# Down projections of the feed-forward blocks turned round: whole-number weights stationary, gated units in two halves moving, transposed back; bank table and written-out order lists

## The chip, the core and the metric

The kernel runs on one core of one Trainium2 chip. The metric is the device time of one execution in microseconds (us), the median of several. The engines are TensorE (PE, with its weight loads as PEld), VectorE (DVE), ScalarE (ACT), GpSimd (POOL) and SyncE (SP), which issues most DMAs. Each engine runs its own instructions in the order in which they are written, and waits at semaphores for the others.

## What is computed

The input x holds 8 sequences ("batches" below) of 256 rows with 128 features. Four residual blocks follow one another, each on a layernorm of x: a first attention without softmax (A), a feed-forward block (F), a causal softmax attention with 16 heads of 64 (B), and the same feed-forward block again (P, with the same weights). Cut down:

```python
x = x + attn_a(layernorm(x))     # sigmoid projections, signed exp(-|dt|) weights, @ V @ Wo
x = x + ffn(layernorm(x))        # "F"
x = x + attn_b(layernorm(x))     # 16 heads, causal softmax, "B"
x = x + ffn(layernorm(x))        # "P"

def ffn(x):                      # w_*: whole numbers from -127 to 127, scaled by 1/127
    gate, up = x @ wg.T, x @ wu.T            # 128 -> 384 each
    return (silu(gate) * up) @ wd.T          # 384 -> 128
```

All is in float32. The down projection, the product with `wd`, is what the change is about.

## The kernel before

**Tiles.** A batch is 256 rows, two tiles of 128 (`T = 2`). After each layernorm the normalised rows are transposed on PE (job `lntA`, `lntF`, `lntB`, `lntP`, line 300) and kept with features on partitions, as a high half in the fp32r format (ACT, line 489) and the rest, the low half (DVE, line 671). fp32r products need one pass of PE over the moving columns for each instruction, so most projections are sums of products of halves: `qkv` (block A) and `qk`, `v` (block B) of three (`split3`, lines 280 to 282), the gate and up products `gF0..2`, `gP0..2` of two, since the whole-number weights are exact in one half (lines 342 and 343). The rest is plain float32, which the trace shows as two PE records for each product: `mean` (313, 315), `vwo` (323), `aout` (331), scores (418, 420), the sums of values (454), `out0/out1` (384), and the down projections `dnF`, `dnP` (line 352). Heads are taken in pairs, `m` from 0 to 63, eight pairs for a batch.

**Down projection.** `gF0..2` give, for a third of the 384 units each, gate and up in one PSUM bank. ACT takes tanh of the gate (512), DVE makes `gated` (676) and `hid` (679). For each of the two row tiles `dnF` then takes the columns of `hid` as the stationary operand, three of 128x128, and streams `wd` (128 columns, float32): six products, twelve records. The result has rows on partitions, and DVE adds it to x straight from PSUM (650).

**Attention B, one pair of heads.** `qk` on PE, DVE adds the bias (722), `scores` on PE, DVE masks and takes the maximum (696, 698), ACT takes exp (543, 545), DVE the inverse of the sums (712), POOL normalises (`norm`, 798), PE transposes the probabilities (432), ACT and DVE copy them out (552, 705), and PE forms the weighted sums (454), two pairs at a time.

**Order.** `order(engine)` gives each engine its list of jobs. It is a table of numbers: steady places per pair of heads (`HEADS`) and per batch (`JOBS`), with places of their own for the first batches (`FIRST`), the last ones (`FINAL`) and single jobs (`ONCE`); the list is sorted by them. Batches overlap: while B of batch b runs, A and F of the next batches and P of the last one are put between its pairs of heads. `hot` and `end` jobs are four products of the identity with itself, that nobody reads.

**Banks.** PSUM has eight banks. Four are fixed for the attention, two for scores and two for transposed probabilities, and the other jobs share four by the table `BANK`: all `qk` use one bank and all `sum` the same one. `take` makes PE wait until the last user of the bank is done (`g_free`); `full` and `freed` are waits for a bank written or emptied.

Of the kernel before, what the change touches and what calls it, by code (L numbers as in the profile page):

```python
# [21 lines left out]
P = 128  # L22
ALU = mybir.AluOpType
# [6 lines left out]
H, A = 16, 64  # L30
# [17 lines left out]
HEADS = {  # L48
    "PE": {"qk": (-1.47, -1.62856), "scores": (0.0, -0.833), "transposes": (1.99091, 1.19991), "sum": (3.2, 3.14491)},
    "ACT": {"exp0": (0.23441, -0.21159), "exp1": (0.28441, -0.20059), "pt0": (2.07727, 1.29991), "sum": (3.3, 3.24991)},  # L50
    "DVE": {"qk": (-0.5119, -0.63388), "mask": (0.708, 0.228), "inverse": (1.29732, 1.34732), "pt1": (2.71379, 2.82508)},
    "POOL": {"norm": (5.06245, 4.32791)},
}
JOBS = {
    "PE": {"lntA": -13.6156, "qkv0": -12.26453, "qkv1": -10.64958, "qkv2": -10.30138, "mean": -10.13088, "vwo": -9.72583,
           "aout": -9.10583, "lntF": -7.70714, "gF0": -6.78825, "gF1": -5.78525, "gF2": -5.72825, "dnF": -4.7632, "lntB": -2.16884,
           "v0": -1.55034, "v2": 1.06591, "v1": 1.20257, "v3": 4.88788, "out0": 10.5084, "out1": 13.1196, "lntP": 14.58389,
           "gP0": 15.43388, "gP2": 15.922, "gP1": 19.74527, "dnP": 23.94389},
    "ACT": {"lntA": -13.17167, "qkv0": -13.0559, "qkv1": -10.76319, "qkv2": -10.2456, "dist": -9.90133, "vwo": -9.70983,
            "lntF": -7.53195, "gF0": -5.89131, "gF1": -5.34525, "gF2": -5.30283, "lntB": -2.36166, "v0": -1.25162, "v2": 1.67502,  # L60
            "v1": 2.21014, "v3": 5.60312, "lntP": 14.41869, "gP0": 15.53771, "gP2": 16.02125, "gP1": 19.2699},
    "DVE": {"lnsA": -21.82637, "lntA": -11.8, "mean": -9.39079, "sign": -9.09363, "aout": -8.43983, "lnsF": -7.98053, "lntF": -6.51241,
            "gF0": -5.20042, "gF2": -4.66206, "gF1": -4.63025, "dnF": -3.78101, "lnsB": -3.68499, "lntB": -1.24016, "out0": 12.0634,
            "out1": 13.89046, "lnsP": 13.97249, "lntP": 15.50477, "gP2": 16.5658, "gP0": 16.76417, "gP1": 20.95233, "dnP": 24.54168},
    "POOL": {"lnsA": -17.39504, "sv": -5.80262, "stdp": -4.98145, "lnsF": -4.33472, "lnsB": 0.17439, "bo": 6.18821, "lnsP": 18.15549},
}
ONCE = {
# [773 lines left out]
```

## Time and profile before

| | us |
|---|---|
| median of 3 runs | 344.57 (344.52 to 344.84) |
| span of the profiled execution | 342.4 |
| what lies around the span (median less span) | 2.2 |
| PE busy | 329.4 |
| DVE busy | 264.8 |
| ACT busy | 231.6 |
| POOL busy | 200.0 |

The profiled execution has no time of its own beside its span; the median is set against that. Matmuls are pipelined, so the busy time of PE counts overlapping ends; how fast it goes is read from the distance between the starts of its instructions in the timeline.

### The profile page before, as it was taken

The numbers are of one execution on the slowest core, as the hardware profiler recorded it, in microseconds if no ns is written. First come the engines' busy times: TensorE is split into PE (matmuls) and PEld (weight loads), VectorE is DVE, ScalarE is ACT, GpSimd is POOL, SyncE is SP. The second block draws the span as 40 slices with busy tenths as digits, with TensorE's granted clock in tenths as the row PEclk, the third lists the DMA queues.
The fourth block names the chain that finished last, engine by engine and source line by source line (L and its number), as shares of the span: only waits on it lengthen the run. The fifth ranks groups of instructions, "written<-read, shape, count | busy, mean of one in ns | idle before, by whom it ended". The sixth has DMA issues, their size and how long they took to land.

```text
span 342.4 us, 10121 instructions
## 1 busy us (share of the span) xinstructions
PE 329.4 (96%) x3344; PEld 284.3 (83%) x3344; DVE 264.8 (77%) x1092; ACT 231.6 (68%) x784; POOL 200.0 (58%) x265
## 2 busy tenths in 40 slices
PE   6899899999999999999999999999999999999985
PEld 5788697779888888889988888888898888888875
DVE  4566799779889798898788788887787886877553
ACT  2544676986788767685786767685787757866711
POOL 4566587477676677557657667634658265444600
PEclk9999999999999999999999999999999999999999
DMA  7800000000000000000000000000000000000001
GB/s 207 278 3 0 3 0 4 2 2 4 0 2 4 2 0 3 17 3 1 2 3 19 0 2 4 15 2 3 3 0 18 2 3 15 3 2 3 16 2 31
DMA packets 6418, 5.83 MB, mean 17 GB/s; under 512 B 864, under 2 KB 5856, under 8 KB 6368
## 3 DMA queue, kind: packets, MB, share of 16 engines
q1 hardware_dynamic: 6080, 4.99, 4.9%
q8 instruction: 27, 0.44, 0.5%
q10 hardware_dynamic: 288, 0.20, 0.2%
q14 instruction: 23, 0.19, 0.2%
HBM read 4.15 MB, written 1.05 MB: 15 GB/s over the span
## 4 chain that ended last, share of the span: by engine, by line
PE 76%; POOL 8%; issue 7%; DVE 5%; ACT 2%; DMA 1%; DVEq 0%; POOLq 0%
PE bank L454 11%; PE bank L280 7%; PE bank L432 7%; PE bank L420 7%; PE bank L384 7%; PE bank L282 6%; PE bank L281 6%; PE bank L418 6%; PE bank L352 5%; PE bank L342 4%; PE bank L343 3%; PE bank L300 2%; POOL prob L798 2%; PE bank L331 2%; POOL wqkv_lo L785 1%
## 5 line engine op out<-in xcount | busy, mean ns | idle before, releaser
L798 POOL TENSOR_TENSOR prob<-prob,row_inv 128x256 f32<-128x256 f32 (+1 forms) x128 | 103.1, 826 | 90.1 <-DVE row_inv L712 90.1
L545 ACT ACTIVATE prob<-neg_s,neg_max 128x256 f32<-128x256 f32 x128 | 63.7, 498 | 0.0
L543 ACT ACTIVATE prob<-neg_s,neg_max 128x128 f32<-128x128 f32 x128 | 50.5, 394 | 17.8 <-DVE neg_max L698 17.2
L698 DVE CUSTOM_DVE_ANT_0 neg_s<-bank,mask 128x256 f32<-128x256 f32 x128 | 53.6, 419 | 0.0
L722 DVE TENSOR_TENSOR qk<-bank,bqk 128x512 f32<-128x512 f32 x64 | 44.0, 688 | 11.9 <-PE bank L282 10.9
L454 PE MATMUL bank<-prob_t,v 128*64 128x256 f32 (+1 forms) x512 | 48.7, 332 | 0.2
L454 PEld LDWEIGHTS bank<-prob_t,v 128*64 128x64 f32 x512 | 32.0, 136 | 19.5 <-ACT prob_t L552 9.7
L696 DVE CUSTOM_DVE_ANT_0 neg_s<-bank,mask 128x128 f32<-128x128 f32 x128 | 36.6, 286 | 13.6 <-PE bank L420 13.1
L552 ACT ACTIVATE prob_t<-bank 128x384 f32<-128x384 f32 x64 | 30.9, 482 | 19.7 <-PE bank L432 18.9
L280 PE MATMUL bank<-rt_hi,wqkv_hi 128*128 128x256 f32 x128 | 39.9, 312 | 0.3
L420 PE MATMUL bank<-qk 64*128 64x256 f32 x256 | 38.5, 377 | 0.0
L432 PEld LDWEIGHTS bank<-ident,prob 64*128 64x128 f32 x768 | 31.8, 139 | 7.4 <-POOL prob L798 0.9
L432 PE MATMUL bank<-ident,prob 64*128 64x64 f32 x768 | 36.0, 226 | 0.4 <-DVE prob_t L705 0.4
L705 DVE COPY prob_t<-bank 128x384 f32<-128x384 f32 x64 | 35.2, 549 | 1.6 <-PE bank L432 1.6
L282 PE MATMUL bank<-rt_lo,wqkv_hi 128*128 128x256 f32 x128 | 35.8, 280 | 0.0
L281 PE MATMUL bank<-rt_hi,wqkv_lo 128*128 128x256 f32 x128 | 35.8, 280 | 0.0
L418 PE MATMUL bank<-qk 64*128 64x128 f32 x256 | 29.9, 310 | 1.1 <-DVE neg_max L698 0.9
L500 ACT ACTIVATE t_qkv<-bank,ga_bias,ga_scale 128x256 f32<-128x256 f32 x24 | 13.4, 562 | 24.4 <-PE bank L282 24.4
L384 PE MATMUL bank<-wo,zt 128*128 128x128 f32 x232 | 28.3, 275 | 0.0
L384 PEld LDWEIGHTS bank<-wo,zt 128*128 128x128 f32 x232 | 27.3, 192 | 0.2
L280 PEld LDWEIGHTS bank<-rt_hi,wqkv_hi 128*128 128x128 f32 x128 | 24.1, 189 | 2.6 <-DVE qk L722 1.2
L418 PEld LDWEIGHTS bank<-qk 64*128 64x128 f32 x256 | 19.6, 187 | 6.7 <-issue 6.5
(145 smaller groups left out, 795.0 us busy)
## 6 DMA issues: line engine op xcount, KB each, us to landing
wqkv<-wqkv_in SPq DMA_DIRECT2D x3, 512.0 KB, 7.1
x<-x_in SPq DMA_DIRECT2D x8, 128.0 KB, 5.7
out<-x SPq DMA_DIRECT2D x8, 128.0 KB, 1.8
wo<-wo_in SPq DMA_DIRECT2D x1, 512.0 KB, 6.8
wa<-wa_in ACTq DMA_DIRECT2D x1, 192.0 KB, 3.0
wg_i<-wg_in SPq DMA_DIRECT2D x1, 192.0 KB, 3.4
wu_i<-wu_in SPq DMA_DIRECT2D x1, 192.0 KB, 3.5
wd_i<-wd_in SPq DMA_DIRECT2D x1, 192.0 KB, 5.0
```

What stands on the lines that cost most here:

```text
L280: nc.tensor.matmul(out, w_hi_ap, r_hi_ap, start=True, stop=False)
L281: nc.tensor.matmul(out, w_lo_ap, r_hi_ap, start=False, stop=False)
L282: return nc.tensor.matmul(out, w_hi_ap, r_lo_ap, start=False, stop=True)
L384: last = nc.tensor.matmul(out[:, 0:D], zt[:, b % 2, u, j * P:(j + 1) * P], wo[:, u, :], start=(u == 0), stop=(u == U - 1))
L418: nc.tensor.matmul(s_banks[e][:, 0:P], qk[half, r, 0, 0:P], qk[half, r, 1, 0:P], start=True, stop=True)
L420: nc.tensor.matmul(s_banks[e][:, P:SC], qk[half, r, 0, P:N], qk[half, r, 1, :], start=True, stop=True).then_inc(s_full, 1)
L432: last = nc.tensor.transpose(t_banks[h][:, at:at + A], prob[half, m % 4, e, j * P:(j + 1) * P], ident[half, half])
L454: last = nc.tensor.matmul(out[half, t + k * P:t + N], v[:, b % 2, k, h * A:(h + 1) * A], prob_t[:, i % 4, e, cols], start=(k == 0), stop=( ...
L543: nc.scalar.activation(prob[:, r, e, 0:P], neg_s[:, m % 2, e, 0:P], ACT.Exp, bias=neg_max[:, q, 2 * e:2 * e + 1], scale=-1.0, accum_out=ro ...
L545: nc.scalar.activation(prob[:, r, e, P:SC], neg_s[:, m % 2, e, P:SC], ACT.Exp, bias=neg_max[:, q, 2 * e + 1:2 * e + 2], scale=-1.0, accum_ ...
L698: nc.vector.tensor_tensor_reduce(out=neg_s[:, m % 2, e, P:SC], in0=S[:, P:SC], in1=mask[:], scale=-SCORE_SCALE, scalar=3e38, op0=ALU.add, ...
L798: nc.gpsimd.tensor_tensor(pr, pr, inv, ALU.mult).then_inc(p_norm, 1)
```

## The change

The down projections of batches 1 to 7 in F and of 0 to 6 in P (14 of 16) are turned round. `wd`, now held in fp32r, is the stationary operand, and `hid`, split in two fp32r halves, moves: three products of 128x256 for the high half and three for the low half. The split is new work: ACT writes `hid_hi` (job `hh`, 768 columns), POOL subtracts and writes `hid_lo` (job `hl`, 768 columns). The result now has features on partitions; ACT copies it out of PSUM (`dnt`, 256 columns), and a new PE job `dbF`/`dbP` transposes it back, two of 128x128. DVE's addition to x is as before, from the bank of `db`. The first of F and the last of P keep the old form, under the name `db` (`DIRECT`). `hid` is made in place, without `gated`.

Every bank of every job now stands in a table (`BANKS`, one digit for each use), the scores, transposes and `hot` jobs too, and `take` holds for all of them. The orders are written out as lists for each engine (`ORDER`), different all over. The last P uses the buffers of F. There are 18 `hot` jobs in place of 28 `hot` and 6 `end`.

```diff
-JOBS = {
-    "PE": {"lntA": -13.6156, "qkv0": -12.26453, "qkv1": -10.64958, "qkv2": -10.30138, "mean": -10.13088, "vwo": -9.72583,
...
+ORDER = {
+    "PE": """
+        lntA.0 hot.0 hot.1 qkv0.0 qkv1.0 qkv2.0 mean.0 hot.2 lntA.1 hot.3 vwo.0 hot.4 qkv1.1 aout.0 qkv0.1 hot.5 hot.6 mean.1
+        lntF.0 hot.7 hot.8 gF2.0 gF1.0 gF0.0 qkv2.1 bo.0 lntA.2 dbF.0 hot.9 qkv2.2 vwo.1 qkv1.2 qkv0.2 aout.1 lntB.0 hot.10
+        hot.11 qk.0 v0.0 qk.1 scores.0 scores.1 lntF.1 qk.2 qk.3 gF1.1 gF0.1 v3.0 gF2.1 v1.0 qk.4 scores.2 scores.3 scores.4
...
+BANKS = {
...
+    "s0": "3116444442011212746107166024553565711005607344543114072352206173",
+    "s1": "0472076114725337263476243276330606300221422060617720267037635360",
...
+DIRECT = {("F", 0), ("P", B - 1)}
...
+        def turn_of(k, b):
+
+            return b + 1 - (k == "F")
+
+        def buffers(k, b):
+
+            return "F" if (k, b) == ("P", B - 1) else k
...
                 elif job in ("dnF", "dnP"):
                     k = job[2]
-                    for c in range(FC):
-                        freed(pe, f"g{k}{c}", b)
+                    pe.wait_ge(hl_s[k], turn_of(k, b))
                     take(job, b)
-                    for j in range(T):
+                    for half in (hid_hi, hid_lo):
                         for c in range(FC):
-                            last = nc.tensor.matmul(out[:, j * D:(j + 1) * D], hid[k][:, c, j * P:(j + 1) * P], wd[:, c, :],
-                                                    start=(c == 0), stop=(c == FC - 1))
+                            last = nc.tensor.matmul(out[:, 0:N], wd[:, c, :], half[k][:, c, :], start=(half is hid_hi and c == 0),
+                                                    stop=(half is hid_lo and c == FC - 1))
+                    last.then_inc(done, 1)
+                elif job in ("dbF", "dbP"):
+                    k = job[2]
+                    if (k, b) in DIRECT:
...
+                    else:
+                        freed(pe, f"dn{k}", b)
+                        take(job, b)
+                        for j in range(T):
+                            last = nc.tensor.transpose(out[:, j * D:(j + 1) * D], dnt[k][:, 0, j * P:(j + 1) * P], ident[:])
                     last.then_inc(done, 1)
...
             def scores(m):
 
                 freed(pe, "qk", m)
-                if m:
-                    pe.wait_ge(s_masked, 2 * m)
+                take("s0", m)
+                take("s1", m)
...
+                elif job in ("hhF", "hhP"):
+                    k = job[2]
+                    for c in range(FC):
+                        freed(act, f"g{k}{c}", b)
+                    if turn_of(k, b) > 1:
+                        full(act, f"dn{k}", b - 1)
+                    nc.scalar.activation(hid_hi[k][:], hid[k][:], ACT.Copy).then_inc(hh_s[k], 1)
+                elif job in ("dnF", "dnP"):
...
+                    nc.scalar.activation(dnt[k][:, 0, :], src[:, 0:N], ACT.Copy).then_inc(free, 1)
...
+                elif job in ("hlF", "hlP"):
+                    k = job[2]
+                    pool.wait_ge(hh_s[k], turn_of(k, b))
+                    if turn_of(k, b) > 1:
+                        full(pool, f"dn{k}", b - 1)
+                    nc.gpsimd.tensor_tensor(hid_lo[k][:], hid[k][:], hid_hi[k][:].bitcast(F32), ALU.subtract).then_inc(hl_s[k], 1)
```

Three places of the order. PE at the start of the program, before (L300 is `lntA.0`, L365 the `hot` jobs, the others are `qkv0`):

```order
L365 MATMUL bank<-ident 128x128 x24
L300 MATMUL bank<-ident,xn_A 128x128 x2
L365 MATMUL bank<-ident 128x128 x4
L280 MATMUL bank<-xt_hi_A,wa_hi 128x256
L281 MATMUL bank<-xt_hi_A,wa_lo 128x256
```

and after (L373 is `lntA.0`, L454 to L456 `hot`):

```order
L373 MATMUL bank<-ident,xn_A 128x128 x2
L454 MATMUL bank<-ident 128x128 x2
L455 MATMUL bank<-ident 128x128
L456 MATMUL bank<-ident 128x128
L454 MATMUL bank<-ident 128x128 x2
L455 MATMUL bank<-ident 128x128
L456 MATMUL bank<-ident 128x128
L355 MATMUL bank<-xt_hi_A,wa_hi 128x256
```

The 24 products ahead of the first transposes are gone; eight stand behind them.

PE about the down projection of F in batch 4 before (L352 is `dnF`, between two `qk`):

```order
L384 MATMUL bank<-wo,zt 128x128 x8
L280 MATMUL bank<-rt_hi,wqkv_hi 128x256
L281 MATMUL bank<-rt_hi,wqkv_lo 128x256
L282 MATMUL bank<-rt_lo,wqkv_hi 128x256
L280 MATMUL bank<-rt_hi,wqkv_hi 128x256
L281 MATMUL bank<-rt_hi,wqkv_lo 128x256
L282 MATMUL bank<-rt_lo,wqkv_hi 128x256
L352 MATMUL bank<-wd,hid_F 128x128 x6
L280 MATMUL bank<-rt_hi,wqkv_hi 128x256
```

and after (L424 is `dnF`, L441 `dbF`; between them a `qk`, behind them the probabilities' transposes L518):

```order
L541 MATMUL bank<-prob_t,v 64x128 x2
L424 MATMUL bank<-hid_hi_F,wd 128x256 x3
L424 MATMUL bank<-hid_lo_F,wd 128x256 x3
L355 MATMUL bank<-rt_hi,wqkv_hi 128x256
L356 MATMUL bank<-rt_hi,wqkv_lo 128x256
L357 MATMUL bank<-rt_lo,wqkv_hi 128x256
L355 MATMUL bank<-rt_hi,wqkv_hi 128x256
L356 MATMUL bank<-rt_hi,wqkv_lo 128x256
L357 MATMUL bank<-rt_lo,wqkv_hi 128x256
L441 MATMUL bank<-ident,dnt_F 128x128 x2
L518 MATMUL bank<-ident,prob 128x64 x12
```

Six products of another shape stand for the six, and the two back transposes follow one `qk` later.

POOL at the split of `hid` in F, batch 4, after (L913 is `norm`, L860 to L878 `lnsA`, L888 `sv`, L900 `hlF`); before, there is no such row:

```order
L913 TENSOR_TENSOR prob<-prob,row_inv 128x2x128
L913 TENSOR_TENSOR prob<-prob,row_inv 128x2x256
L900 TENSOR_TENSOR hid_lo_F<-hid_F,hid_hi_F 128x768
L913 TENSOR_TENSOR prob<-prob,row_inv 128x2x128
L913 TENSOR_TENSOR prob<-prob,row_inv 128x2x256
L860 TENSOR_TENSOR rstd_A<-var_A,minus_half 128x2
```

`hlF` stands between the `norm` of two pairs of heads, and the second of them waits for it.

## Rows read from the trace of the kernel before

**Rows 1.** The page: busy time of each engine, then 40 equal slices of the span.
```profile
PE 329.4 (96%) x3344; PEld 284.3 (83%) x3344; DVE 264.8 (77%) x1092; ACT 231.6 (68%) x784; POOL 200.0 (58%) x265
...
PE   6899899999999999999999999999999999999985
...
PEclk9999999999999999999999999999999999999999
```

**Rows 2.** Windows, PE alone: stretch, length, busy (instructions), granted clock, DMA share, GB/s.
```profile
60.00:308.00 248.00, 247.48 (x2613) 1.00 0.02 5
```

**Rows 3.** Windows, all engines: PE, PEld, DVE, ACT, POOL busy, then as above.
```profile
193.30:231.60 38.30, 38.30 (x402) 33.25 (x401) 31.20 (x129) 28.07 (x98) 24.32 (x32) 1.00 0.02 5
326.00:342.40 16.40, 11.57 (x96) 10.60 (x94) 7.93 (x24) 2.68 (x7) 0.72 (x1) 1.00 0.06 17
```

**Rows 4.** Timeline of PE about dnF.4: start, length, instruction, count.
```profile
195.57 1.50 PE L352 MATMUL bank<-wd,hid_F 128*128 128x128 f32 x12
196.82 0.36 PE L280 MATMUL bank<-rt_hi,wqkv_hi 128*128 128x256 f32 x1
197.03 0.28 PE L281 MATMUL bank<-rt_hi,wqkv_lo 128*128 128x256 f32 x1
197.15 0.28 PE L282 MATMUL bank<-rt_lo,wqkv_hi 128*128 128x256 f32 x1
```

**Rows 5.** Timeline of PE: two transposes of 128x128, aout, the next qk.
```profile
214.35 0.39 PE L300 MATMUL bank<-ident,xn_P 128*128 128x128 f32 x2
214.57 1.06 PE L331 MATMUL bank<-vwo,stdp 128*128 128x128 f32 x8
215.38 0.37 PE L280 MATMUL bank<-rt_hi,wqkv_hi 128*128 128x256 f32 x1
```

**Rows 6.** Groups by line and shape: count, busy, mean ns, idle time before.
```profile
L785 POOL TENSOR_TENSOR wqkv_lo<-wqkv,wqkv_hi 128x512 fp32r<-128x512 f32 x6 | 7.6, 1287 | 0.7 <-DVE xn_B L615 0.7
L524 ACT ACTIVATE wqkv_hi<-wqkv 128x512 fp32r<-128x512 f32 x6 | 3.6, 623 | 0.0
L489 ACT ACTIVATE xt_hi_P<-bank 128x256 fp32r<-128x256 f32 x8 | 3.1, 382 | 9.6 <-PE bank L300 9.4
```

**Rows 7.** Waits: who waited for whom, us in total, times, longest.
```profile
POOL prob L798 <- DVE row_inv L712: 90.1, 57, 4.4
```

**Rows 8.** Timeline: the last pair's scores on PE, and its normalisation on POOL.
```profile
317.02 0.49 PE L418 MATMUL bank<-qk 64*128 64x128 f32 x4
...
321.50 1.61 POOL L798 TENSOR_TENSOR prob<-prob,row_inv 128x256 f32<-128x256 f32 x2 [0.54 <-DVE row_inv L712]
```

**Rows 9.** Windows, PE alone, inside the first 24 hot products; columns as in rows 2.
```profile
2.90:3.90 1.00, 1.00 (x6) 1.00 0.93 264
...
4.90:5.90 1.00, 1.00 (x11) 1.00 0.84 252
```

**Rows 10.** Timeline, batch 0's chain and batch 1's mean: DVE and POOL.
```profile
12.18 0.75 DVE L635 TENSOR_SCALAR less<-tq,ntk 128x256 f32<-128x256 f32 x2
30.79 1.56 DVE L635 TENSOR_SCALAR less<-tq,ntk 128x256 f32<-128x256 f32 x2
...
14.37 0.81 POOL L770 TENSOR_TENSOR xb<-x,boa 128x256 f32<-128x256 f32 x1
15.27 0.94 POOL L791 TENSOR_SCALAR stdp<-signed 128x512 f32<-128x512 f32 x1
30.43 1.28 POOL L785 TENSOR_TENSOR wqkv_lo<-wqkv,wqkv_hi 128x512 fp32r<-128x512 f32 x1 [0.72 <-DVE xn_B L615]
```

**Rows 11.** Timeline of PE: lntA.0, lntB.0, the second pair's scores, lntP.7.
```profile
6.63 0.41 PE L300 MATMUL bank<-ident,xn_A 128*128 128x128 f32 x2 [0.44 <-DVE xn_A L615]
...
30.41 0.44 PE L300 MATMUL bank<-ident,xn_B 128*128 128x128 f32 x2
...
39.79 0.49 PE L418 MATMUL bank<-qk 64*128 64x128 f32 x4 [0.94 <-DVE neg_max L698]
...
332.82 0.44 PE L300 MATMUL bank<-ident,xn_P 128*128 128x128 f32 x2 [1.08 <-DVE xn_P L615]
```

More of the change, by code:

```diff
@@ L43 @@
 BIG = 1e30
[L48 to L52, printed above, removed]
-}
-JOBS = {
-    "PE": {"lntA": -13.6156, "qkv0": -12.26453, "qkv1": -10.64958, "qkv2": -10.30138, "mean": -10.13088, "vwo": -9.72583,
[L56 to L66, printed above, removed]
@@ new lines @@
+BANKS = {
+    "lntA": "51315605",
+    "qkv0": "15612257",
+    "qkv1": "77315641",
+    "qkv2": "26704630",
+    "mean": "12536726",
+    "vwo": "64761224",
+    "aout": "11142604",
+    "bo": "5",
+    "lntF": "06653573",
+    "gF0": "37203426",
+    "gF2": "45422673",
+    "gF1": "02644713",
+    "dbF": "71536147",
+    "lntB": "05174423",
+    "v1": "06565532",
+    "qk": "6103475323055467264574754747130452375345651647573151564250546145",
+    "v0": "35167174",
+    "s0": "3116444442011212746107166024553565711005607344543114072352206173",
+    "s1": "0472076114725337263476243276330606300221422060617720267037635360",
+    "v3": "13653451",
+    "t0": "6230235630412053022137541514237167663776751350420561121215173427",
+    "t1": "1351570727664502133450160647073242474040062761657643764147031565",
+    "dnF": "04524055",
+    "sum": "0000050000030706060501020001040202010304000700010001050102060706",
+    "v2": "64302267",
+    "out0": "63731140",
+    "out1": "35571723",
+    "lntP": "45452633",
+    "gP0": "00132611",
+    "gP2": "12345734",
+    "gP1": "12524047",
+    "dnP": "0627340",
+    "dbP": "71344730",
+    "hot": "020000012024000001",
@@ L120 @@
 }
 def order(engine):
-    steps = []
-    for name, at in HEADS[engine].items():
-        steps += [(m + at[m % 2], name, m) for m in range(LAST) if name != "sum" or m % 2]
-    for name, at in JOBS[engine].items():
-        first = FIRST[engine].get(name, ())
-        final = FINAL[engine].get(name, ())
-        places = list(first) + [U * b + at for b in range(len(first), B - len(final))] + list(final)
-        steps += [(place, name, b) for b, place in enumerate(places)]
-    for name, at in ONCE[engine].items():
-        steps.append((at, name, 0))
@@ L135, in order, with bank_of, users @@
-    return [(name, n) for _, name, n in sorted(steps)]
-LAST_BANK = {"out0": 4, "out1": 5, "lntP": 6, "gP0": 4, "gP1": 5, "gP2": 6}
-def bank_of(job, n):
-    return LAST_BANK[job] if n == B - 1 and job in LAST_BANK else BANK[job]
+    jobs = []
+    for place in ORDER[engine].split():
+        name, n = place.split(".")
+        jobs.append((name, int(n)))
+    return jobs
+def bank_of(user, n):
+    return int(BANKS[user][n])
+DIRECT = {("F", 0), ("P", B - 1)}
+def users(job, n):
+    if job == "scores":
+        return [("s0", n), ("s1", n)]
+    if job == "transposes":
+        return [("t0", n), ("t1", n)]
+    if job in ("pre0", "pre1"):
+        return [(job.replace("pre", "out"), B - 1)]
+    return [(job, n)]
@@ L147, in bank_turns @@
 def bank_turns():
     turns, count = {}, [0] * 8
-    for name, n in order("PE"):
-        if name in ("pre0", "pre1"):
-            name, n = name.replace("pre", "out"), B - 1
-        if name in BANK and (name, n) not in turns:
-            count[bank_of(name, n)] += 1
-            turns[name, n] = count[bank_of(name, n)]
+    for job, n in order("PE"):
+        for user in users(job, n):
+            if user not in turns:
+                count[bank_of(*user)] += 1
+                turns[user] = count[bank_of(*user)]
@@ L271, in _ @@
             for b in range(B):
-                freed(sp, "dnP", b)
+                freed(sp, "dbP", b)
                 sp.dma_start(out_view[:, b * T:(b + 1) * T, :], x[:, b * T:(b + 1) * T, :]).then_inc(stored, 16)
@@ L289, in side @@
             def side(job, b):
-                out, done, _ = home(job, b) if job in BANK else (None, None, None)
+                out, done, _ = home(job, b) if job in BANKS else (None, None, None)
                 if job.startswith("lnt"):
@@ L646, in side @@
                     nc.vector.tensor_tensor(x[:, ts, :], src[:, 0:N].rearrange("p (j d) -> p j d", d=D), xb[:, b % 2, :, :], ALU.add).then_inc(free, 1)
-                elif job in ("dnF", "dnP"):
+                elif job in ("dbF", "dbP"):
                     src, _, free = home(job, b)
@@ L690, in mask_max @@
                 for e in range(2):
-                    S = s_banks[e]
-                    dve.wait_ge(s_full, 2 * m + e + 1)
+                    S, _, free = home(f"s{e}", m)
+                    full(dve, f"s{e}", m)
                     if m >= 2:
```

260 lines of the change are left out of this document (168 added, 92 removed), and 13 rows, old and new, of tables (FINAL, ONCE).

## The prediction

> **What bounds the kernel now.** I read the page first. PE is busy for 96% of the span, in nearly every slice, at the full granted clock, and no other engine passes 77% [rows 1]. The windows by stretch say the same of the long middle: between 60 and 308 us PE lacks 0.5 us of 248 [rows 2], while in one batch's stretch of 38.3 us DVE works 31.2, ACT 28.1 and POOL 24.3 [rows 3]. So in the middle each us of PE work taken away is a us of time, as long as the others keep pace. Only the two ends have another limit. In the head, batch 0 has to go through blocks A and F before any heads can start (its `lntB.0` stands at 30.41 [rows 11]), and PE is filled with `hot` products. In the tail, from 326 us, PE is busy 11.6 of 16.4 us [rows 3]: the last P is a chain through all engines.
>
> **PE's prices** are distances between starts. A float32 down projection takes 1.25 us to the next start, and the first fp32r product behind it 0.09 more than its like (0.21 against 0.12) [rows 4], so 1.34 in all. An fp32r product of 256 columns takes 0.12 [rows 4]. Two transposes of 128x128 take 0.22 [rows 5]. `aout`, eight float32 records, takes 0.81, with the switch behind it 0.9 [rows 5].
>
> **Part 1, the turned down projections.** New cost of one: 6 x 0.12 = 0.72, and 0.22 for the transposes back. Of the 14 turned, 13 lie ahead of the tail (F 1 to 7, P 0 to 5), and 12 of their `db`; the others (`dnP.6`, `dbP.5`, `dbP.6`) lie in the tail in time in which PE waits for the last P. The sum: 13 x (0.72 - 1.34) = -8.1, and 12 x 0.22 = +2.6: **-5.5 us**. Bounds: if each `db` also brings a switch of 0.09, or one each way, it is -4.4 or -3.3; a gain beyond -5.5 needs a cheaper product than the like ones of `qk`, and no row has that. I take -5.5 since the float32 job that went had its switch too.
>
> **Part 2, what is moved ahead.** In the new order `lntA.2`, `vwo.1`, `aout.1` and `qkv0..2.2` stand ahead of `lntB.0`, where before they stood behind it (where PE is the limit) and `hot` products stood ahead. By the same prices: 0.22, four records of the down projection's kind 0.45 (4/12 of 1.34), 0.9, and 9 x 0.12 = 1.08. **-2.7 us**, hidden by the chain of batch 0. If that cover is too short, up to all of it comes back.
>
> **Part 3, banks.** Before, the second pair's scores waited 0.94 us until the first pair's bank was masked [rows 11]. The table now gives them banks of their own, and the two stand side by side: **-0.9 us**. In the middle PE had no waits worth counting [rows 2], so free banks bring nothing more there by themselves. `take` is one semaphore wait as before. Side by side, scores with scores and transposes with transposes, may save switches: adding up all prices of both lists from `lntB.0` to the last `out1` gives up to 1.0 us more for the new order than parts 1 and 2. No row shows two scores in a row; I leave it out of the sum and keep it for the range (0 to -1.0).
>
> **Part 4, the head.** Is `lntB.0` still at 30.4? For it: POOL now does batch 1's layernorm ahead of `sv.0`, so `stdp.0` is not held back by it. It began at 15.27, right behind batch 1's `xb` of 0.81 that ended at 15.18 [rows 10]: an estimated 0.6 earlier. Against it: DVE now does `mean.1`, whose `less` alone takes 0.75 to 1.56 [rows 10], between the norm and the low half of `lntF.0`, in part in time in which it waited before: an estimated +0.3 to +1.1. It also does `lnsA.2` and `bv` while the gates' tanh runs: about +0.5, half of which the three gates, now side by side, give back. And PE starts cold, next. Sum between -0.5 and +2; I take **+0.9 us**, the middle.
>
> The clock in the head: PE's first 24 `hot` products took some 0.17 us each before 3.9 us (6 in 1 us) and half of that at 4.9 (11 in 1 us), although the granted clock is given as 1.00 over both [rows 9]. So the array began at its lower level, 1.2 GHz, and rose while these ran. Without them it rises only behind `lntA.0`, at 6.63 or later [rows 11]: the transposes, eight `hot` and the first `qkv` at double price. The `hot` that stood between `qkv0` and `qkv1` is gone, which pays for most of it: 0.3 to 0.5, in the +0.9.
>
> **Part 5, work for the others.** ACT: `hh` has 768 columns; 512 took 0.62 and 256 0.38 [rows 6], so 0.86; `dnt` 0.38. 14 x 1.24 = 17 us over the run, 2.2 a batch: 28.1 to 30.3 of 37.3 us. POOL: `hl` by the like subtraction of 512 columns at 1.29 [rows 6] is 1.9 us; 14 of them 27 us, 3.5 a batch: 24.3 to 27.8. DVE is as before, 31.2 of 37.3. None reaches PE. What counts is what is queued behind. On POOL it is the next pair's `norm`, for which transposes on PE wait. POOL had waited 90.1 us in 57 places for the inverse [rows 7], 1.6 each: one `hl` eats that. The whole way from scores to the end of the normalisation was 317.02 to 323.11 = 6.1 us [rows 8]; with a full `hl` in front, 8.0. By the prices above, summed along the new list, PE has 7.2 to 16 us of other work between scores and transposes at the 13 pairs whose `norm` follows an `hl`, eleven of them over 8.3. From the last gate to `dn` PE has 5.4 us or more, against 0.8 on DVE (two steps of 256 columns, as the two `less` [rows 10]) + 0.9 + 1.9 = 3.6 and the semaphores. `dn` to `db` has 0.7 at its shortest, against 0.38 for the copy and two semaphores: just enough. I cost part 5 at **0**, at 0 to +5 for the range.
>
> **The shared port.** When POOL split a weight, `less` on DVE took 1.56 in place of 0.75 [rows 10]. The Trainium skill ("SBUF — State Buffer", section "Who interferes with whom") says that DVE in certain modes, or with two SBUF inputs, and POOL share one port pair as an exclusive lock, the loser waiting for the whole instruction; the trace agrees by these two rows. By that rule `hl` can hold DVE for up to 1.9 us with `qk` and `mask` behind. DVE has three such instructions a batch (two `less`, `signed`), and `hl` runs 3.5 of 37 us, so about 0.3 meet in a batch, some 0.3 us on an engine with 6 us to spare. It changes the bounds of part 5, not the sum.
>
> **Tail.** The last P keeps its form. `pre0` now stands ahead of the last `sum`, a mere exchange on PE. `dnP.6` (0.7) replaces an `end` in the wait between `lntP.7` (332.82 [rows 11]) and its gates. 0.
>
> **Sum.** -5.5 - 2.7 - 0.9 + 0.9 = -8.2 us: span 342.4 to 334.2, with the 2.2 around it **336.4 us**.
>
> **Rivals.** (a) The clock stays low through the head: with fewer `hot` the array is at work perhaps two thirds of the time there, and batch 0's own PE jobs (some 4.5 us at full clock from `mean.0` to `lntB.0`) take double: +4.5, of which 0.4 is counted and some falls into waits: +3.5, 339.9. For it: rows 9. Against it: in the tail PE was busy 70% of the time [rows 3] and the clock held. The Trainium skill ("TensorE: Matmul & The Clock Gate", section "What's actually happening") says that throttled is the default and activity releases it; by that the start is cold, as rows 9 show. (b) The in-order engines give part of it back: 14 splits with 0.3 us of PE wait each, +4.2: 340.6. For it: DVE at 84% and ACT at 81% of the time are no longer slack for every job. Against it: the distances above. (c) The same orders save the 1.0 us of switches, and the head comes out at -0.5 or better: -1.0 - 1.4 or a bit more, some 333.7. (d) The turned product doesn't do what it says: six products with their switches and the copy cost 1.3 after all. Then part 1 is 0 and it is 341.9. Nothing speaks for it, since the `qk` products of rows 4 have the same types. (e) **Slower than before:** POOL becomes the chain. Each `hl` is late by the wait for `hh` behind exps on ACT, and PE stands for all of the 1.9 us at each of 14 places and 0.3 after `dn`: +30 at most; it turns slower from 0.6 us at each (8.2 / 14). At 0.8 each and nothing else it is +3 over before: 347.6. Against it is the room of 7 to 16 us.
>
> **How the numbers follow.** The forecast, 334.5 to 338.5, gets 0.52; (c) 0.14; (a) 0.13; (b) 0.15; (d) 0.02; (e) 0.04. Leaving out the lower end of (c) and the upper of (b), (d) and (e), the range is 332.0 to 341.5. A change within 0.2% (0.7 us), about what a measurement of this kernel can tell from none, is at the edge of (b) and (d) only: faster 0.94, same 0.02, slower 0.04.
>
> **What the new profile would show.** Part 1: line 424 with 0.12 between starts, 0.7 for six, and line 441 0.22. Part 2 and 4: `lntB.0` (line 373, xn_B) at 31.3, with the jobs of batch 2 ahead of it. Part 3: the first two scores back to back, no wait. Part 5: `hl` at 1.9, `hh` at 0.86, PE lacking no more than a us or so between 60 us and the last sums. (a) would show in records of the head at double length, (b) and (e) in transposes waiting for POOL's `prob`. I am wrong if the middle has PE waits of over 2 us, or `lntB.0` is later than 33.

## The result, and the profile after

| | us |
|---|---|
| before, median of 4 runs | 344.64 (344.52 to 344.84) |
| after, median of 4 runs | 345.88 (345.76 to 346.28) |
| after / before | 1.0039, 95% interval 1.0025 to 1.0053 |
| span of the profiled execution of after | 344.0 |

The change makes the kernel 0.4% slower; 336.4 was forecast. In three of the kernels below one execution took far longer than its like (627.97 us in e1, 1294.51 in e2, 1712.59 in e5); the medians contain it, the ratios do not. The page of after, busy times and slices, beside rows 1:

```profile
PE 320.7 (93%) x3224; PEld 273.5 (79%) x3224; DVE 271.6 (79%) x1092; ACT 245.9 (71%) x812; POOL 225.4 (66%) x279
...
PE   2879999999999999999999989999999999999994
...
PEclk9989999999999999999999999999999999999999
```

PE is busy for 8.7 us less, but that is not the saving that was priced: the `hot` and `end` products alone fell from 19.5 to 11.2 us. DVE is busy for 6.8 us more, with as many instructions. The third slice of the clock (17 to 26 us) is lower than before. The window of rows 2, PE alone, and one about that slice (length, busy, granted clock, DMA share, GB/s):

```profile
60.00:308.00 248.00, 241.70 (x2511) 1.00 0.02 5
20.00:30.00 10.00, 8.12 (x58) 0.83 0.01 2
```

In the middle PE now lacks 6.3 us of 248, where it lacked 0.5. These are 27 waits, 16 of them over 0.1 us, the longest 1.25 and 1.23. The price of the turned product itself was right: six records at 0.12, as the timeline of PE at `dnF.1` shows (the next job may start at 49.57 + 0.35 and the switch).

```profile
49.11 0.62 PE L424 MATMUL bank<-hid_hi_F,wd 128*128 128x256 f32 x3
49.57 0.51 PE L424 MATMUL bank<-hid_lo_F,wd 128*128 128x256 f32 x3
```

The second pair's scores now follow the first at once (37.61 behind 36.81), so the wait of rows 11 is gone too. Where DVE's time went, its groups say (count, busy, mean ns):

```profile
L737 DVE TENSOR_SCALAR less<-tq,ntk 128x256 f32<-128x256 f32 x16 | 9.2, 617 | 0.3
...
L707 DVE TENSOR_SCALAR var_P<-mv_P 128x2 f32<-128x2 f32 x7 | 5.1, 735 | 0.2
L707 DVE TENSOR_SCALAR var_A<-mv_A 128x2 f32<-128x2 f32 x8 | 3.6, 452 | 0.3
L707 DVE TENSOR_SCALAR var_F<-mv_F 128x2 f32<-128x2 f32 x9 | 3.0, 331 | 0.3
```

`var`, which adds epsilon to two variances, is an instruction on two elements. Before, the same groups had 170, 169 and 169 ns, and `less` 419. All `var` together took 13.5 us in place of 6.0, and `less` 9.2 in place of 6.0; other work of DVE is shorter. The timeline of after about one of them, DVE, POOL and PE:

```profile
168.06 1.05 DVE L707 TENSOR_SCALAR var_P<-mv_P 128x2 f32<-128x2 f32 x1
169.03 0.17 DVE L819 RECIPROCAL row_inv<-row_sum 128x4 f32<-128x4 f32 x1
...
169.61 1.48 DVE L737 TENSOR_SCALAR less<-tq,ntk 128x256 f32<-128x256 f32 x2
...
167.48 1.61 POOL L913 TENSOR_TENSOR prob<-prob,row_inv 128x256 f32<-128x256 f32 x2
169.28 1.66 POOL L913 TENSOR_TENSOR prob<-prob,row_inv 128x256 f32<-128x256 f32 x2 [0.18 <-DVE row_inv L819]
170.90 0.76 POOL L860 TENSOR_TENSOR rstd_P<-var_P,minus_half 128x2 f32<-128x2 f32 x1
...
172.67 0.97 PE L518 MATMUL bank<-ident,prob 64*128 64x64 f32 x24 [1.25 <-DVE neg_max L804]
```

`var_P` starts while POOL normalises, and ends when that ends, 169.09. The inverse of the next pair's sums stands behind it; POOL waits for it; `less` is then held through the second `norm`; masks stand behind `less`; and PE stands 1.25 us before its transposes. A longer case behind `hlF`: `var_A` at 198.37 took 1.62 us, `hlF` ran from 198.15 for 1.82. "Held up" below means this: an instruction of DVE that takes longer beside one of POOL. Sixteen of the 32 `var` are held up, for 8.3 us in all, and each ends within 0.03 us after an instruction of POOL: eleven with a `norm` (5.2 us), three with `hl` (2.5), the others with the split of a weight and with `xb`.

The kernel before had this too, twice, in the group that the means above leave out (`var_B`, 226 ns). DVE and POOL at the first of the two; the other is `var_B` at 86.53, 0.37 us:

```profile
53.32 0.43 DVE L603 TENSOR_SCALAR var_B<-mv_B 128x2 f32<-128x2 f32 x1
...
52.11 1.61 POOL L798 TENSOR_TENSOR prob<-prob,row_inv 128x256 f32<-128x256 f32 x2 [0.47 <-DVE row_inv L712]
```

### The profile page after: what moved, and what is told of

Read it like the earlier page. It is cut to its first block, busy times and chain, and to the rows that moved or that the text cites. A ratio compares the mean times of both kernels' runs of the same rounds, so it can differ in the third digit from the quotient of the medians.

```text
span 344.0 us, 10014 instructions
## 1 busy us (share of the span) xinstructions
PE 320.7 (93%) x3224; PEld 273.5 (79%) x3224; DVE 271.6 (79%) x1092; ACT 245.9 (71%) x812; POOL 225.4 (66%) x279
## 3 DMA queue, kind: packets, MB, share of 16 engines
HBM read 4.15 MB, written 1.05 MB: 15 GB/s over the span
## 4 chain that ended last, share of the span: by engine, by line
PE 73%; DVE 12%; issue 7%; ACT 4%; POOL 3%; DMA 1%; DVEq 0%; ACTq 0%; POOLq 0%
PE bank L541 11%; PE bank L355 7%; PE bank L518 7%; PE bank L469 6%; PE bank L356 6%; PE bank L357 6%; PE bank L506 6%; PE bank L503 5%; PE bank L415 4%; PE bank L416 3%; PE bank L424 3%; PE bank L404 2%; PE bank L373 2%; DVE neg_s L804 1%; DMA x<-x_in 1%
## 5 line engine op out<-in xcount | busy, mean ns | idle before, releaser
L913 POOL TENSOR_TENSOR prob<-prob,row_inv 128x256 f32<-128x256 f32 (+1 forms) x128 | 103.2, 833 | 59.3 <-DVE row_inv L819 59.1
L802 DVE CUSTOM_DVE_ANT_0 neg_s<-bank,mask 128x128 f32<-128x128 f32 x128 | 36.5, 285 | 11.8 <-PE bank L506 11.7
L541 PEld LDWEIGHTS bank<-prob_t,v 128*64 128x64 f32 x512 | 32.7, 136 | 16.4 <-issue 6.2
L829 DVE TENSOR_TENSOR qk<-bank,bqk 128x512 f32<-128x512 f32 x64 | 42.1, 679 | 4.0 <-PE bank L357 3.9
L355 PE MATMUL bank<-rt_hi,wqkv_hi 128*128 128x256 f32 x128 | 38.2, 298 | 0.5 <-DVE rt_lo L773 0.3
L812 DVE COPY prob_t<-bank 128x384 f32<-128x384 f32 x64 | 33.8, 549 | 4.0 <-PE bank L518 3.8
L518 PEld LDWEIGHTS bank<-ident,prob 64*128 64x128 f32 x768 | 29.2, 139 | 9.0 <-issue 5.4
L655 ACT ACTIVATE prob_t<-bank 128x384 f32<-128x384 f32 x64 | 29.3, 484 | 8.9 <-PE bank L518 8.7
L518 PE MATMUL bank<-ident,prob 64*128 64x64 f32 x768 | 33.0, 226 | 2.6 <-DVE neg_max L804 1.9
L503 PEld LDWEIGHTS bank<-qk 64*128 64x128 f32 x256 | 21.3, 186 | 7.1 <-issue 3.7
L645 ACT ACTIVATION_READ_ACCUMULATOR prob<-neg_s,neg_max 128x1 f32 x128 | 24.6, 192 | 0.0
```

Source lines behind the costliest of these rows:

```text
L355: nc.tensor.matmul(out, w_hi_ap, r_hi_ap, start=True, stop=False)
L503: nc.tensor.matmul(home(f"s{e}", m)[0][:, 0:P], qk[half, r, 0, 0:P], qk[half, r, 1, 0:P], start=True, stop=True)
L518: last = nc.tensor.transpose(out[:, at:at + A], prob[half, m % 4, e, j * P:(j + 1) * P], ident[half, half])
L541: last = nc.tensor.matmul(out[half, t + k * P:t + N], v[:, b % 2, k, h * A:(h + 1) * A], prob_t[:, i % 4, e, cols], start=(k == 0), stop=( ...
L645: nc.scalar.activation(prob[:, r, e, 0:P], neg_s[:, m % 2, e, 0:P], ACT.Exp, bias=neg_max[:, q, 2 * e:2 * e + 1], scale=-1.0, accum_out=ro ...
L913: nc.gpsimd.tensor_tensor(pr, pr, inv, ALU.mult).then_inc(p_norm, 1)
```

## Experiments

Theory A: DVE's small instructions are held up by POOL where the new orders let them meet. Theory B: the halves on ACT and POOL ate the gain. The head was examined apart. Each kernel was timed beside the kernel before (medians 344.45 to 344.64). "New" below is the changed kernel.

**e1. Old down projections in the new orders.**

```diff
-DIRECT = {("F", 0), ("P", B - 1)}
+DIRECT = {(k, b) for k in "FP" for b in range(B)}
+SKIP = ("dnF", "dnP", "hhF", "hhP", "hlF", "hlP")      # left out of every order list
...
-                        if (k, b - 1) in DIRECT:
-                            full(dve, f"db{k}", b - 1)
-                        else:
-                            dve.wait_ge(hl_s[k], turn_of(k, b - 1))
+                        full(dve, f"db{k}", b - 2)      # hid has two buffers of each kind
```

> The new orders and the new bank table, with every down projection in its old direct form (at the place of the job that turned the result back): no high and low halves, no copy back. By the prices of the prediction PE has 5.5 us more to do than in the changed kernel (13 x 1.34 against 13 x 0.72 + 12 x 0.22). Theory A, VectorE's small instructions are held up by GpSimd because of where the new orders put them: the turned form is innocent and is missed, 345.9 + 5.5, about 350 to 351. Theory B, the halves on ScalarE and GpSimd (0.84 and 1.83 us at each of 14 places) ate the gain: taking them out gives back up to 7.6 us of PE's small waits, 343 to 345, no slower than the changed kernel.

Measured: 353.71 (ratio 1.0262, 1.0244 to 1.0279). The turned form is missed by 7.6 to 7.8 us, more than its price and more than theory A gave (350 to 351). B as a whole falls: taking the halves out gives nothing back. The new orders with the old form are 9 us slower than the kernel before.

**e3. The low half cut short.**

```diff
-nc.gpsimd.tensor_tensor(hid_lo[k][:], hid[k][:], hid_hi[k][:].bitcast(F32), ALU.subtract)
+w = N if turn_of(k, b) == 1 else 2
+nc.gpsimd.tensor_tensor(hid_lo[k][:, :, 0:w], hid[k][:, :, 0:w], hid_hi[k][:, :, 0:w].bitcast(F32), ALU.subtract)
```

> The changed kernel, in which GpSimd takes the low half of two columns in each block of 256 instead of all (after the first batch of each kind): the low half of the product is left out, the instruction and its place stay, and its 1.83 us go (12 of 14). Theory A: only the three hold-ups of VectorE behind these instructions go, 3.4 us on VectorE, about 1 us of time: 345. Theory B: norm is no longer late, 341 to 343.

Measured: 343.70 (0.9983, 0.9973 to 0.9992), 2.2 below new. It lies between the two expectations; e13 decides. `var` is still held up for 6.5 us in its trace, where the stretch from `lntB.0` to `lntP.7` is 1.7 us shorter than in new.

**e5 and e5b. `var` as a reduction.**

```diff
-nc.vector.tensor_scalar(var[c][:], mv[c][:, :, 1], EPS, None, ALU.add)
+nc.vector.tensor_reduce(var[c][:], mv[c][:, :, 1:3], mybir.AxisListType.X, ALU.add)   # mv[..., 2] holds EPS
```

> The changed kernel, in which the one small instruction that adds epsilon to the two variances (128x2, 0.17 us alone, up to 1.62 behind GpSimd) is a reduction over the variance and a stored epsilon. The Trainium skill (SBUF - State Buffer, section Who interferes with whom) says that a reduction never takes the shared port pair. Theory A: its mean falls from 0.45 to 0.74 us to about 0.2, 8.3 us of VectorE's hold-ups go, and of PE's 7.6 us of small waits 2 to 5: 341 to 344. Theory B: VectorE has room anyway, 345.5 to 346.

> The kernel of e5 again, for its profile: 341 us as there. Theory A: var takes 0.15 to 0.25 us at all its places, and VectorE's busy time is 8 us below the changed kernel's 271.6. If theory A is wrong and the reduction only moved things, var still has places of over 0.5 us.

Measured: 341.00 (0.9887, 0.9862 to 0.9912) and, the same kernel again, 340.50 (0.9882, 0.9868 to 0.9897): 4.9 and 5.4 us below new, by an instruction of 0.17 us. Two groups of e5b, and DVE at the place shown above:

```profile
L709 DVE TENSOR_REDUCE var_A<-mv_A 128x2 f32<-128x4 f32 x8 | 1.3, 158 | 0.3
...
L709 DVE TENSOR_REDUCE var_P<-mv_P 128x2 f32<-128x4 f32 x7 | 1.1, 157 | 0.2
```

```profile
167.06 0.16 DVE L709 TENSOR_REDUCE var_P<-mv_P 128x2 f32<-128x4 f32 x1
167.16 0.18 DVE L821 RECIPROCAL row_inv<-row_sum 128x4 f32<-128x4 f32 x1
...
166.41 3.27 POOL L915 TENSOR_TENSOR prob<-prob,row_inv 128x256 f32<-128x256 f32 x4
...
170.38 0.96 PE L518 MATMUL bank<-ident,prob 64*128 64x64 f32 x24
```

POOL works through both pairs in one piece, across `var_P`, and PE's wait of 1.25 us is gone. The Trainium skill ("SBUF — State Buffer", "Who interferes with whom") says that a reduction never contends with GpSimd; the trace agrees, 157 to 158 ns in all four groups.

PE alone from `lntB.0` to `lntP.7`, in before, in new and in e5b:

```profile
30.41:332.82 302.41, 298.40 (x3106) 1.00 0.02 5
...
32.87:333.54 300.67, 292.95 (x3033) 1.00 0.02 4
...
33.04:328.57 295.53, 291.98 (x3033) 1.00 0.02 4
```

The prediction took 9.1 us off this stretch (parts 1 to 3). The change took off 1.7, and with `var` as a reduction it is 6.9, of which 6.4 is work of PE.

**e10. The same form in the kernel before.**

> The kernel before with the reduction of e5 in place of its own addition of epsilon: a control. Its own orders keep this instruction away from GpSimd's work (0.6 us of hold-ups in all on VectorE, against 8.3 in the changed kernel). Theory A: nothing to win, 344.0 to 344.6. If the reduction were simply the cheaper form of layer norm, it would bring several us here too: 340 to 342.

Measured: 343.98 (0.9981, 0.9972 to 0.9991): 0.6 us. The gain of e5 is thus no virtue of the form by itself; the old orders keep all but two of the meetings away.

**e12. The same form in e1.**

> The kernel of e1 (new orders and banks, every down projection direct) with the reduction of e5. If the hold-ups come from the orders alone, the gain is the one that e5 had with the turned form: 353.7 - 4.5 to 5.5, so 348.2 to 349.2. If the halves on GpSimd have a good share in them: 350 to 352.

Measured: 351.71 (1.0200, 1.0185 to 1.0216), only 2.0 below e1, in the range that was given for a good share of the halves. In e1, without them, `var` takes 10.0 us in all and is held up for 4.7 of them, against 13.5 and 8.3 in new. The smaller gain has a second part that stays open: PE lacks 7.7 us of the window 60 to 308 in e12, so other waits are late in its place.

**e13 and e16. The halves again, once DVE is free.** Both build on e9 (below). e13 has e3's edit, e16 also cuts the high half:

```diff
-nc.scalar.activation(hid_hi[k][:], hid[k][:], ACT.Copy)
+nc.scalar.activation(hid_hi[k][:, :, 0:w], hid[k][:, :, 0:w], ACT.Copy)
```

> As e9 (339.4), where VectorE's small instruction is no longer held up, with the low half on GpSimd cut to two columns of each block after the first batch of each kind (the low half of the product is left out, the instruction stays). In the changed kernel itself the same cut gave 2.2 us (e3). If that was the halves' own weight in GpSimd's row (norm late, transposes late), it is there again: 337.2 to 338.2. If it came by way of the hold-ups of VectorE, nothing is left of it: 339.0 to 339.5.

> As e13, with the high half on ScalarE cut in the same way (both halves of the product are then left out after the first batches, PE's work stays): 0.84 us less on ScalarE at 12 places. If ScalarE's part costs time of its own, 0.3 us or more below e13; if not, within 0.3 us of it.

Measured: 339.53 and 340.47, against 339.44 for e9. Nothing is left of e3's 2.2 us, so `hl` cost time only as one of the things that hold up DVE. Taking ACT's part out brings nothing either; e16 fits neither of its expectations, and why it is 0.9 slower isn't settled. Theory A stands, with the halves as one part of the hold-ups; B falls.

**e11. `less` in an accumulating form too.**

```diff
-nc.vector.tensor_scalar(less[:, j, :], tq[:, b % 2, :], ntk[:, b % 2, j:j + 1], 0.0, ALU.add, ALU.is_lt)
+nc.vector.tensor_scalar(less[:, j, :], tq[:, b % 2, :], ntk[:, b % 2, j:j + 1], None, ALU.is_lt, ALU.add, accum_out=count[:, j:j + 1])
```

(`ntk` is stored with the other sign, and `dist` takes that back by a scale of -1.)

> As e9, and the two comparisons of a batch in the form that also adds up its results: same values, one more short record each. The Trainium skill (SBUF - State Buffer, section Who interferes with whom) says that this form does not enter the modes that take both ports. If so, no comparison is held up any more (now 0.59 us on average, up to 1.2 each), each takes 0.3 to 0.4, and the 3 us of hold-ups are exchanged for 16 x 0.15 = 2.4 us of steady work on VectorE: within 0.5 us of e9. If they are still held up: slower than e9 by 0.5 to 1.5.

Measured: 339.92 (0.9853, 0.9833 to 0.9874), same as e9. `less` takes 475 to 480 ns at all 16 places, not the 0.3 to 0.4 expected, with 83 for the extra record, against 503 on average in e9 with the hold-ups. `signed` behind it takes 894 in place of 818. No gain in all.

**e2, e2b and e14. The turned form in the old orders.** e2 and e2b put 13 of them into the lists of before, e14 only P 0 to 3 and 5.

> The kernel before, its orders and its banks, with 13 of its down projections turned (F 1 to 7, P 0 to 5); the new jobs are put in at the times that the trace of before leaves free, everything else stands where it stood. Theory A (the loss comes from the new orders): the turned form brings what PE's prices say, 13 x (0.72 - 1.34) + 13 x 0.22 = -5.2 us, less a us for the places that no search has smoothed: 339.5 to 341. Theory B (the halves ate it): 344 to 347.

> As e2, which came to 382.8 us because GpSimd stood up to 8.6 us before the layer norm of block B, whose data came later than its place in the row, and PE 2.6 us at a down projection whose bank the gate product in front of it still held. Here the gate product gP1 follows the down projection on all engines, and the layer norm of B stands one us later on GpSimd. If these two places were all of it, the turned form brings its 5 us less a us or two in the old orders: 340 to 343. If the old orders have no room for 1.83 us more on GpSimd between scores and transposes (about 6 us there, against 7 and more in the new orders), each of the 13 halves stands on PE's path for one to two us: 350 to 365.

> The kernel before, its orders and banks, with only five down projections turned: P 0 to 3 and 5, which before had 12 to 15 us between their last gate and the product; the low half stands on GpSimd in the longest gap there (1.6 to 3.5 us of waiting in the trace of before), nothing else is moved. e2b (13 turned, 374.7 us) was slow either because the turned form with its halves doesn't fit the old orders at all, or because the F half's longer chain pushed layer norm and all behind it. If the first: each of the five costs a us or two, 348 to 355. If the second: the prices hold, 5 x (1.34 - 0.72 - 0.22) = 2 us less than before: 342.2 to 343.5.

Measured: 382.79, 374.71 and 344.97 (1.0010, 1.0000 to 1.0019). In e2b POOL's waits are led by

```profile
POOL prob L868 <- DVE row_inv L776: 75.2, 44, 5.1
POOL rstd_B L816 <- DVE var_B L663: 15.1, 5, 4.1
```

so the places by hand were bad ones: POOL stood before B's layernorm with norms behind it. Both runs lie outside all that was expected; they say nothing of the form, only how dear a wrong place is in orders that are in step. e14, which lies outside its two ranges too, says more. `dnP.2` before, and in e14 (PE, ACT):

```profile
217.24 1.50 PE L352 MATMUL bank<-wd,hid_P 128*128 128x128 f32 x12
218.67 0.58 PE L432 MATMUL bank<-ident,prob 64*128 64x64 f32 x12
219.09 0.44 PE L418 MATMUL bank<-qk 64*128 64x128 f32 x4
```

```profile
217.41 0.51 PE L378 MATMUL bank<-hid_hi_P,wd 128*128 128x256 f32 x3
217.76 0.52 PE L378 MATMUL bank<-hid_lo_P,wd 128*128 128x256 f32 x3
218.21 0.59 PE L474 MATMUL bank<-ident,prob 64*128 64x64 f32 x12
218.84 0.41 PE L395 MATMUL bank<-ident,dnt_P 128*128 128x128 f32 x2
219.19 0.49 PE L460 MATMUL bank<-qk 64*128 64x128 f32 x4
...
218.31 0.39 ACT L581 ACTIVATE dnt_P<-bank 128x256 f32<-128x256 f32 x1 [0.22 <-PE bank L378]
```

From the product to the scores it was 1.43 + 0.42 = 1.85 us and is 0.80 + 0.63 + 0.35 = 1.78. The product saves 0.63, as priced. Of this the back transposes take 0.35 (0.22 and a switch), and 0.2 is PE's wait for ACT's copy, since one job of 0.42 between `dn` and `db` doesn't cover it. So a turned projection saves next to nothing here (0.07). Where the copy is covered, 0.28 to 0.4 us is left by these numbers, 0.63 less 0.35 or 0.22; that is an estimate. For the whole of e14, `var`, still in its old form, adds a little: it is held up for 1.4 us, against 0.5 before, since two more meet `hlP`.

**e6, e8, e9, e15 and e17. The head.** After, DVE and POOL, then PE:

```profile
20.04 2.34 DVE L737 TENSOR_SCALAR less<-tq,ntk 128x256 f32<-128x256 f32 x2
22.30 0.41 DVE L773 TENSOR_TENSOR xt_lo_F<-bank,xt_hi_F 128x256 fp32r<-128x256 f32 x1
...
19.69 2.54 POOL L893 TENSOR_TENSOR wqkv_lo<-wqkv,wqkv_hi 128x512 fp32r<-128x512 f32 x2 [0.72 <-DVE xn_F L717]
...
22.86 0.39 PE L415 MATMUL bank<-xt_hi_F,wg 128*128 128x256 f32 x1 [1.88 <-DVE xt_lo_F L773]
23.05 0.41 PE L416 MATMUL bank<-xt_lo_F,wg 128*128 128x256 f32 x1
23.26 0.41 PE L415 MATMUL bank<-xt_hi_F,wu 128*128 128x256 f32 x1
...
32.87 0.38 PE L373 MATMUL bank<-ident,xn_B 128*128 128x128 f32 x2
```

`less` is held from 20.04 to 22.3 by the split of a weight, batch 0's gates wait 1.88 us for the low half behind it, and after that idle time PE's records stand 0.21 apart in place of 0.12. The edits, on new (e6) and on the kernel of e5:

```diff
-lnsF.0 mean.1 lntF.0 lnsA.2          (DVE; e6, e8, e9, e15, e17)
+lnsF.0 lntF.0 mean.1 lnsA.2
-lntA.0 hot.0                         (PE; e8)
+hot.18 hot.19 hot.20 hot.21 hot.22 hot.23 lntA.0 hot.0
-"hot": "020000012024000001"          (e8)
+"hot": "020000012024000001777777"
+pe.wait_ge(consts, 1)
+for _ in range(24):                  (PE, ahead of the list; e15, e17)
+    nc.tensor.transpose(bank[7][:, 0:P], ident[:], ident[:])
-"hot": "020000012024000001"          (e17)
+"hot": "020000011024000001"
```

> The changed kernel with one exchange on VectorE: the low half of batch 0's transposed lntF.0 ahead of mean.1 with its two comparisons, which stood behind GpSimd's split of a weight until 22.2 us. If this is the head's loss: PE's idle 1.9 us before the gates goes, the clock does not fall at 22.9 us, lntB.0 stands at 30.5 to 31.5 in place of 32.87, and the time is 344 to 345. If the comparisons only move behind another job of the chain (mean.1's results, sign.1, aout.1): lntB.0 at 32.5 to 33 and 345.5 to 346.

> The changed kernel with the reduction of e5, the exchange of e6, and six hot products (24 transposes) ahead of lntA.0 as before. If the losses are separate they add up: 341.0 - 1.5 - 0.4 = 339 us. If PE's small waits in the middle take up what the head gives: 340.5 to 341.

> The changed kernel with the reduction of e5 and the exchange of e6, without hot products at the start (in e8 these 24 transposes, four to 1.24 us at 0.21 each, lasted to 9.04 us and held up lntA.0 by 2.4 us). If the gains of e5 (5.4 us) and e6 (0.4 in time, 1.0 at all points of its profile) add up: 339.3 to 340.0, lntB.0 at 31.8 to 32. If the middle takes it up again: 340.3 to 340.7.

> As e9, with 24 transposes back to back at PE's start, without semaphores between them, as before (in e8 the same number in six jobs with semaphores took to 9.04 us). The prediction put the cold start at 0.3 to 0.5 us. If it is on batch 0's chain: lntB.0 at 31.2 to 31.4 and 338.9 to 339.2. If the chain's other waits hide it: 339.3 to 339.5, lntB.0 at 31.65.

> As e15 (338.07), with one digit of the bank table changed: hot.8 uses bank 1 in place of bank 2, which mean.1 still holds. In e9's trace hot.8 waited 0.99 us for mean.1 to be read and the gates stood behind it at 22.19, although the low half that they need was ready at 21.25. If the gates are on batch 0's chain: they start 0.8 us earlier, and the time is 337.2 to 337.6. If the bias copy, the gate activations or the weights on GpSimd are what lntB.0 waits for: no change, 337.9 to 338.2.

Measured: e6 345.52, e8 340.30, e9 339.44 (0.9849, 0.9833 to 0.9865), e15 338.07 (0.9812, 0.9798 to 0.9827), e17 338.21. In the profiled execution of e6, its fastest (344.53), `lntB.0` stands at 31.75 and `lntP.7` 1.0 earlier than in new; the medians show 0.4. That fits neither of its two cases as a whole. e9 gives 1.1 on e5b and lies in its first range. e8, a little under its second range, lost that again: its six jobs with semaphores took 1.24 us each and ended at 9.04, in front of `lntA.0`. In the profiled execution of e15, its slowest (338.85), the 24 take 0.21 each to 7.12, 0.4 past the time at which `lntA.0` could start, yet the first `qkv` products behind it go at the full level:

```profile
1.95 5.38 PE L548 MATMUL bank<-ident 128*128 128x128 f32 x24 [1.95 <-POOL ident L854]
7.12 0.63 PE L373 MATMUL bank<-ident,xn_A 128*128 128x128 f32 x2
...
8.97 0.28 PE L356 MATMUL bank<-xt_hi_A,wa_lo 128*128 128x256 f32 x1
9.09 0.28 PE L357 MATMUL bank<-xt_lo_A,wa_hi 128*128 128x256 f32 x1
```

and the time is 1.4 us lower, below both of its ranges. Only 0.6 of that lies in the kernel's span: e9's four spans are 336.7 to 336.8, three of e15's 336.1 to 336.3. The other 0.8 is time around the span, 2.5 to 2.8 us in e9 and 1.8 in e15; why it falls when PE has work at the start isn't known. In e17, with the same start, the 24 are done sooner (in this execution the full level came at 4.7 us):

```profile
1.95 4.15 PE L548 MATMUL bank<-ident 128*128 128x128 f32 x24 [1.95 <-POOL ident L854]
6.65 0.41 PE L373 MATMUL bank<-ident,xn_A 128*128 128x128 f32 x2 [0.55 <-DVE xn_A L722]
```

Its gates start at 20.77 without a wait, but `bo` behind them then waits 1.02 us for DVE's copy of the bias: no change. e15 is the fastest kernel of this study, 1.9% below before.

## Why the prediction was wrong

Starting from 345.88, the runs give 5.4 us to `var` (e5b), 1.1 to the place of `lntF.0` on DVE (e9), 1.4 to PE's start (e15). That is 338.07, 1.7 above the forecast. The spans can be laid against the forecast's 334.2 by stretch:

| us | forecast | new | e5b | e17 |
|---|---|---|---|---|
| start to `lntB.0` | 31.3 | 32.9 | 33.0 | 31.0 |
| `lntB.0` to `lntP.7` | 293.3 | 300.7 | 295.5 | 295.6 |
| `lntP.7` to the end | 9.6 | 10.4 | 9.6 | 9.6 |

So 7.4 of new's 9.8 us too many lie in the long middle, and 5.1 of these are gone with `var` as a reduction. Of the 2.2 that stay, 1.8 are work of PE: it is 6.4 less, not the 8.2 of parts 1 and 2. Waits make up the rest. In e9's window (columns as in rows 2) PE lacks 2.25 us where before lacked 0.5, but outside it, up to `lntP.7`, PE waits less than before (1.3 us, against 3.5).

```profile
60.00:308.00 248.00, 245.75 (x2566) 1.00 0.02 5
```

- **What bounds the kernel:** right. PE was the limit, and each wait of PE in the middle is time.
- **Parts 1 to 3, PE's prices:** right within 2.2 us of 9.1. Most of the work did go. The bound of one switch for each `db` (1.1 us in all) was the better value where `db` stands by itself (e14: 0.35 for it in place of 0.22).
- **Part 5, work for others at 0:** right for what it priced. `hl` took 1.83 and `hh` 0.84 us, close to the estimates, and with `var` as a reduction nothing is won by cutting them short (e13, e16). Its load of a batch is a little low, since a batch of the middle has two splits: 2 x 1.24 is 2.5 us for ACT, not 2.2, and 2 x 1.9 is 3.8 for POOL, not 3.5.
- **The shared port: this step failed.** It named the mechanism from two rows, counted 0.3 us in a batch (2.4 over the run) on DVE, and put it at 0 in the sum. Measured: `var` alone is held up for 8.3 us on DVE and costs 5.4 us of time (e5b). The step took only `hl` against `less` and `signed`. It left out `var`, four in a batch, which has the same form as `less`, and the 103 us of `norm` on POOL, which stands behind 5.2 of the 8.3 us. None of its rows showed that meeting, but the trace of before has it twice, at `var_B`; the new order made it sixteen meetings with all of POOL's work. A hold-up ends with POOL's instruction, so 0.17 us became up to 1.62. And "an engine with 6 us to spare" was no cover: an inverse or a mask directly behind the held instruction passes it on to `norm` and to PE. Rival (b), in-order engines giving back 0.3 us at each split, had a like sum (4.2, against 5.4) with the wrong place, and its 340.6 is 5.3 below the measured time. The text's own sign, PE waits of over 2 us in the middle, came true.
- **Part 4, the head: mis-sized.** `lntB.0` at 32.87, not 31.3. `less` ahead of `lntF.0`'s low half was priced at +0.3 to +1.1 and became 2.34 us long; PE's records are at the lower level behind the idle time that followed (granted clock 0.83 from 20 to 30 us). The cold start, priced at 0.3 to 0.5, was worth 0.6 in the span; the 2.2 us around the span, which the sum took as fixed, moved by 0.8 with it. With all this undone `lntB.0` stands at 31.04 (e17, in which `hot.8` has another bank too). Two slips of the working change little: +0.9 is not the middle of its bounds of -0.5 and +2, which is 0.75; and the first `hot` products of before stand 0.21 us apart, not 0.17.
- **Tail 0:** right. From `lntP.7` to the end it is 9.6 us before and 10.4 in the profiled execution of new, but 9.6 in e6 and in e9, whose tail is the same.

What stays open: why the new orders with the old form are 9 us slower than before and keep 7.7 us of PE waits even in e12, what the rest of the 1.8 us of PE's work is, and whether any placing of all 13 turned products pays in the old orders.

## What to carry to other kernels

When a change reorders two engines that share a port, list every instruction of the one that can be held, by kind and not by length, and lay it against every long instruction of the other in the new order. Search the old trace for meetings by the longest of each kind, not by a few rows: here `var_B` showed 0.43 us where its like took 0.17, and the price of two such meetings says nothing of an order that has sixteen. A tiny instruction in a holdable form in front of a hand-over can be dear; another form of it can cost no more (0.16 us) and needs no search (here 5.4 us for one line). And price a turned product with the jobs that must cover its copy back.

## What was not expected of the hardware

- A `tensor_scalar` of 128x2 elements, 0.17 us alone, took up to 1.62 us beside POOL's subtraction of 768 columns and 1.05 beside a `norm`; as a `tensor_reduce` it took 0.157 to 0.158 us at all 32 places.
- PE's cold start isn't shown by the granted clock, which is 1.00 from 2 to 7 us in e15 while 24 transposes take 0.21 us each. With 24 back to back from 1.95 us the records shorten to 0.11 at 4.7 us in e17, at 4.8 before, and at 7.8 in the profiled execution of e15; without them it came at 9.4 (new) or 11.1 (e9); as six jobs with gaps, at about 11.7 (e8).
- The level fell again near 22 us only in some executions of one kernel: e15's spans are 336.1, 336.2 and 336.3 at a mean clock of 1.000 and 337.1 at 0.995. In new, PE had idled 1.88 us just before, and in e15's execution 0.98; in the profiled execution of e3 it idled 1.89 and the records stayed at 0.12. The length of that idle time alone doesn't decide it.
